# Context loads queued ahead of the last store of expert answers, and a merge moved one step earlier

## The reference, cut to what matters

```python
x = x + L0_xattn(layernorm(x), ctx, Wq, Wk, Wv, Wo, bo)            # 16 heads of 64
x = x + L0_ffn(layernorm(x), gate_w, w1, b1, w2, b2, sw1, ...)     # one of 2 experts, and a shared one
x = x + L1_xattn(layernorm(x), ctx, ctx, mask)                     # softmax(x ctx^T / 16) ctx, one head
x = x + L1_ffn(layernorm(x), weight_int8, weight_scale, bias)      # int8 product of 256 x 256
```

## Time and profile before

| | us |
|---|---|
| median of 3 runs | 957.77 |
| lowest, highest | 957.72, 958.77 |
| the profiled execution | 958.77 |
| its span | 956.0 |

### The profile page before, as it was taken

The page is one execution under the profiler, slowest core; times in us unless marked ns, Lnnn a source line. Parts: engine busy times, 40 slices in busy tenths (PEclk is TensorE's granted clock), DMA queues, the critical chain, the costliest instruction groups (busy, mean ns, idle before and its releaser), DMA issues.

```text
span 956.0 us, 19821 instructions
## 1 busy us (share of the span) xinstructions
PE 903.7 (95%) x6730; PEld 794.5 (83%) x6730; DVE 623.0 (65%) x1634; ACT 525.6 (55%) x1258; POOL 268.2 (28%) x337
## 2 busy tenths in 40 slices
PE   5889999999999999999999999998989999998864
PEld 4779888898888988889898898887878999996643
DVE  6766666767667676676766767665654666348777
ACT  4655565555655556555565555654742555446633
POOL 1323333333333333333433334333100000041214
PEclk9999999999999999999999999999999999999985
DMA  9230000000000000000000000000550142265502
GB/s 290 97 106 17 2 18 5 21 16 5 16 5 21 16 5 16 5 21 16 5 16 5 21 14 7 0 5 9 162 190 20 54 169 85 63 193 163 155 6 77
DMA packets 29459, 50.56 MB, mean 53 GB/s; under 512 B 2480, under 2 KB 24080, under 8 KB 27648
## 3 DMA queue, kind: packets, MB, share of 16 engines
q1 hardware_dynamic: 27888, 46.42, 15.6%
q0 software_dynamic: 1536, 3.67, 1.3%
HBM read 41.83 MB, written 8.26 MB: 52 GB/s over the span
## 4 chain that ended last, share of the span: by engine, by line
PE 88%; DVE 7%; ACT 2%; issue 2%; DMA 1%; POOL 0%; DVEq 0%
PE bank L1648 27%; PE bank L1677 10%; PE bank L1841 9%; PE bank L1696 9%; PE bank L1861 8%; PE bank L1662 8%; PE bank L1630 6%; PE bank L1717 5%; PE bank L1950 2%; PE bank L1968 1%; DVE norm_stats L1023 1%; PE bank L1811 1%; PE bank L1609 1%; PE bank L1957 1%; DMA x_all<-in_x 1%
## 5 line engine op out<-in xcount | busy, mean ns | idle before, releaser
L664 POOL TENSOR_TENSOR probs<-probs,row_rcp 112x375 f32<-112x375 f32 x256 | 202.4, 813 | 415.8 <-DVE row_rcp L1118 415.3
L784 ACT ACTIVATE probs<-bank,neg_max 112x375 f32<-112x375 f32 x256 | 144.4, 570 | 69.0 <-DVE neg_max L1112 68.9
L1677 PE MATMUL bank<-ident,probs 112*125 112x112 f32 x768 | 129.1, 277 | 2.3 <-DVE probs_t L1123 2.3
L1677 PEld LDWEIGHTS bank<-ident,probs 112*125 112x125 f32 x768 | 113.8, 187 | 18.2 <-issue 3.3
L1112 DVE TENSOR_REDUCE neg_max<-bank 112x1 f32<-112x375 f32 x256 | 123.3, 539 | 7.6 <-PE bank L1662 7.5
L1123 DVE COPY probs_t<-bank 125x336 f32<-125x336 f32 x128 | 64.7, 506 | 70.1 <-PE bank L1677 66.8
L756 ACT ACTIVATE k_parts<-bank 128x376 fp32r<-128x376 f32 x128 | 62.1, 485 | 69.3 <-PE bank L1648 69.3
L1648 PE MATMUL bank<-ctx_hi,wk_hi 128*128 128x376 f32 x256 | 97.2, 380 | 2.3 <-DVE k_parts L1103 1.5
L759 ACT ACTIVATE v<-bank 125x512 f32<-125x512 f32 x96 | 57.4, 598 | 57.2 <-PE bank L1648 57.1
L1696 PE MATMUL bank<-probs_t,v 125*64 125x112 f32 x1536 | 87.7, 263 | 0.6 <-ACT probs_t L772 0.6
L1696 PEld LDWEIGHTS bank<-probs_t,v 125*64 125x64 f32 x1536 | 74.0, 137 | 16.9 <-issue 16.7
(11 more groups left out here) (208 smaller groups left out, 1877.0 us busy)
## 6 DMA issues: line engine op xcount, KB each, us to landing
stage<-in_ffn_up SPq DMA_DIRECT2D x6, 1024.0 KB, 5.4
stage<-in_ffn_down SPq DMA_DIRECT2D x6, 1024.0 KB, 7.5
ctx_raw<-in_ctx_t SPq DMA_DIRECT2D x16, 375.0 KB, 3.4
ring_late<-in_ctx_t SPq DMA_DIRECT2D x10, 375.0 KB, 6.8
ring_late<-in_ctx_n SPq DMA_DIRECT2D x10, 375.0 KB
routed<-xn SPq DMA_DIRECT2D x1, 2240.0 KB, 11.1
rows_in<-routed SPq DMA_DIRECT2D x5, 448.0 KB, 6.1
answers<-y_rows SPq DMA_DIRECT2D x10, 224.0 KB, 2.7
```

The costliest lines, as they stand in the source:

```text
L664: eng.tensor_tensor(probs[s][:, :], probs[s][:, :], row_rcp[:, s:s + 1].broadcast_to([S, C]), ALU.mult).then_inc(probs_ready, 1)
L784: eng.activation(probs[r][:, :], SCORE_BANKS[i][0:S, 0:C], ACT.Exp, bias=neg_max[:, r:r + 1], accum_out=row_sum[:, r:r + 1]).then_inc(exp_ ...
L1677: t = eng.transpose(turn_bank(i, project)[0:CJ, j * S:(j + 1) * S], probs[QUAD * v + i][:, j * CJ:(j + 1) * CJ], ident[0:S, 0:S])
```

## The change

There are two moves; no operation is added or taken away. SyncE's `load_ring` of t = 3 to 6 now stands ahead of the wait for the last slot and of `store_rows(4)`, right behind `load_ring(2)`. In VectorE's last segment `norm3_merge(0)` and `norm3_stats(0)` stand in step 2, behind its `hid_lo`, and no longer in step 3; the moments and the first five small operations stay in step 3.

```diff
@@ SyncE @@
             load_ring(1)
             eng.wait_ge(down_ready, FIRST_SLOT + SLOTS - 1)
             store_rows(3)
-            load_ring(2)
+            for t in range(2, 2 + len(ring_late)):
+                load_ring(t)
             eng.wait_ge(down_ready, FIRST_SLOT + SLOTS)
             store_rows(4)
-            for t in range(3, 2 + len(ring_late)):
-                load_ring(t)
@@ VectorE @@
                     if s == NS - 1:
-                        if m == 3:
+                        if m == 2:
                             norm3_merge(0)
                             norm3_stats(0)
+                        if m == 3:
                             norm3_moments(0)
                             norm3_ops(0, 0, 5)
```

## The result

The changed kernel takes **968.03 us** (median of six, 963.14 to 971.12) beside **957.50 us** for the kernel before (median of six, 956.69 to 958.77).

The account below looks back on a forecast made before the run. TensorE's matmul queue was taken as the bound, busy 95% of 956.0 us. Merge +4.5 and `hid_lo` +0.6 gave +5.1, clock counted 0, on the median 957.8: 962.9 us; range 959.5 to 968.0.

Parts of the forecast that it names:

- What bounds the kernel: Whole kernel: TensorE busy 95% of 956.0 us, time won or lost where it stops or VectorE sets the pace.
- the held store: SyncE's queue: last store waits behind ring loads, landing about 851.2 instead of 839; merge begins 4.5 us later.
- The ring time of 4.8 us: SyncE's queue: time per ring for rings 3 to 6 without gathers, ends 4.5 and 6.2; last byte at 850.3 us.
- one more `hid_lo`, +0.6: VectorE, between merge and ready normalisation: one more `hid_lo` of 0.62 us, adding 0.6 us.
- I count 0: TensorE behind its new stop: low clock costs nothing, since some 24 matmuls (5 us) end ahead of the delayed `xn`.
- the stated end of 1.7: TensorE behind its stop: at most 1.7 us lost to low clock, counted only in the high end.
- A: Rival, SyncE's queue: the store is not held up; gain of at most 0.75 us, 957.0 to 957.8, chance 0.07.
- B: Rival, SyncE's queue: rings drain fast enough, 3.5 us each; +0.4 us, 958.2, chance 0.06.
- C: Rival: SyncE blocks on stores or rings take 6 us, clock loss uncovered; +9 to +12, 967 to 970, chance 0.05.
- D: Rival, the attention: runs quicker with less traffic beside it, faster by more than 0.2%; chance 0.02.
- 0.75 us: Last feed-forward segment: the earlier merge, if its data were there, shrinks TensorE's two gaps by 0.75 us at best.
- B's sum of +0.4: Merge at m=2 under fast ring drain: group 0 a few tenths behind 853.3, plus one more `hid_lo`, sum +0.4.

Follow-up runs that it names:

- e1_rings_only: The kernel before with only the loads of rings 3 to 6 moved ahead of the last store, merge left at m=3: 963.63 us, ratio 1.0053.
- e3_store_on_act: The changed kernel with the last two `answers` stores issued by ScalarE on its own queue: 959.68 us, ratio 0.9998.
- e8: The changed kernel, nothing altered, run again on another chip: 967.11 us, ratio 1.0077 against the kernel before.
- the filler: The changed kernel plus 22 matmuls with unread results ahead of the waiting `down`; measured twice, 961.91 us (ratio 1.0037) and 962.67 us (ratio 1.0066).
- e4: The changed kernel, nothing altered, run again beside the first experiments: 963.76 us, ratio 1.0045 against the kernel before.
- e6: The changed kernel with only rings 3 and 4 ahead of the last store, merge at m=2: 963.36 us, ratio 1.0033.
- e9: The changed kernel, nothing altered, run again on a third chip: 962.55 us, ratio 1.0057 against the kernel before.
- e10: The changed kernel plus 22 matmuls with unread results in TensorE's stop, on the third chip: 962.67 us, ratio 1.0066.
- e11: The kernel before plus 14 matmuls with unread results in TensorE's 2.89 us gap that ended at 710.73: 957.26 us, ratio 1.0002.
- e12: The kernel before with rings 3 and 4 moved ahead of the last store, merge left at m=3: 957.87 us, ratio 1.0003.
- e13a to c: The changed kernel, nothing altered, three profiled executions on a fourth chip: 961.55, 966.11 and 961.46 us.
- e14: The kernel before with rings 3 to 6 ahead of the last store and `ctx_n` loads cut into 112 and 13 partitions: 958.60 us, ratio 0.9993.
- e2: The kernel before with only the merge and statistics of group 0 moved to m=2: 957.55 us, ratio 0.9993.
- e5: The changed kernel plus 22 matmuls with unread results ahead of the `down` that waits: 961.91 us, ratio 1.0037.
- e7: The changed kernel with each `ctx_n` load cut into 112 and 13 partitions, merge at m=2: 961.81 us, ratio 1.0018.

## Why the prediction was right and where it was not

**What bounds the kernel; the held store (edit 1): right, and shown.** e1_rings_only has the whole loss, e3_store_on_act, which takes the store alone out of SyncE's queue, has none. The trace of after follows the forecast closely: the store issued at 840.93 (840.6 forecast), the first gather at 852.37 (852.2), the merge at 858.80 (858.8), `shift` at 865.25 (865.5), TensorE's stop of 4.47 us ahead of a `down` (about 5). The ring time of 4.8 us, taken as a choice between 4.5 and 6.2, was right for this execution; that the choice hit so closely was in part luck, since e8 has 2.4 us more.

**The term "one more `hid_lo`, +0.6": a little too large.** From merge to `shift` the trace has 6.45 us against 6.11 before, +0.34. In the times it is smaller still: the changed kernel and e1_rings_only differ by 0.13 us.

**The step that failed in the sum: "I count 0" for the clock, and all behind `shift`.** The claim was that the "some 24 matmuls" behind the stop end ahead of the delayed `xn` even at the low clock, and that from the merge on everything keeps its spacing. They don't: in the trace of after these 24 take 6.58 us (from 862.04 until TensorE turns `xn` at 868.62), with the filler, at full clock, 5.16 (860.86 to 866.02), and `xn` lies ready at 867.53. So TensorE comes last there, and the first `neg_max` is 0.60 later. The filler gives 9.26 back, in both of its runs, which shows the cause. I had the row that says so the earlier trace rows and argued it away. In e8, with 6.8 us low, the clock costs 1.26 us, which the stated end of 1.7 covers; the rest of its 2.7 is the pause of ScalarE, of which the forecast had nothing. On top of it came 0.8 us behind the first `neg_max` in this execution. In the other traces that stretch has two values, whatever the kernel: 86.3 to 86.5 us (before, e4, e6, e8, e9, e10, e11, e12, e13a to c, e14) and 86.9 to 87.2 (after, e1, e2, e3, e5, e7). So the 0.8 is not put down to the change; what decides between the two I don't know. The attention does keep its spacing, as claimed: its last `neg_max` follows the first by 50.4 or 50.5 us in before, after, e1 to e8 and e10, of either kind, so the 0.8 lies in the last block.

**The median: +10.5 where the trace has +6.2. This part is not settled.** The clock's 0.60 is a small part of the miss: of the 5.4 us between forecast and median, some 4 lie between the profiled execution and the median. On the chips of the experiments the same program lost 5.5, 8.2 and 5.2 us of the median; ratios 1.0045, 1.0077 and 1.0057. The forecast of +5.1 is a ratio of 1.0053, which lies inside the intervals of all three, and outside that of the first measurement alone. Two quantities vary, as the table shows, and the forecast had only part of either. One is the drain of the queue: the ends "4.5 and 6.2" a ring covered it, but the traces of before can't show how it varies. The other is low clock far ahead of the change. For the first measurement there are 25 executions of the changed kernel with a mean clock each: the median is 0.978 (0.982 in the profiled one, which is among the fastest) and the span falls by 0.8 us for each 0.001 of clock, so about 3 us of the extra go with the clock. It is not shown that the change lowers it: in the groups of e4, e8 and e9 the changed kernel's median clock is 0.980 to 0.982, that of the kernel before 0.981. At the clock of 0.982 its spans are 962.2 to 965.2; on the chips of e4 and e9 they are 960.4 to 962.3 and on that of e8 963.4 and 963.5. So up to another 3 us are not clock, and look as a drain like e8's would. Neither is shown for those executions, which have no trace of their own but one.

A part of it was in my own starting point. 957.5 is what six executions of the kernel before gave; on the four chips of the experiments its medians were 958.3, 959.0, 957.4 and 959.2. And its profiled execution carried a pause of ScalarE (1.68 us idle before the relu at 851.53, while the next relu's matmuls were done too, since it follows at 852.58 with no gap), so its stretch from store to `shift` is 37.89, where e11_before_filler and e12_two_ahead_merge3 have 36.7. Against those the changed kernel loses 5.5 us there, not 4.35. Taken up to the first `neg_max`, the traces whose store was not held (e2, e3, e11, e12, e14) need 45.8 to 46.2 us from the store, those of the changed kernel 51.1 to 52.5, and e8 56.5: a loss of 5 to 6.5 us, and in e8 of 10.5. So a late gather and a pause like those of e8 would make about the +10.5 of the first measurement; that its executions had them is not shown.

**The rivals.** A (not held) is refuted by the trace and e3. B (fast drain) did not happen here, but a fast drain does take most of the loss away: with edit 1 alone all of it (e14_split_merge3), with both edits, which is what B was about, not all in the median (e7_split_ctx_n, 1.0018 [0.9998, 1.0038]). The 145 GB/s that the Trainium skill's figure gave for five engines (DMA: Bandwidth & Descriptors, Specifications) are not reached: 119. C (+9 to +12) is where the median fell, but not by C's mechanism as far as the traces show. SyncE did block at the stores (4.12 us) and the clock was not covered (0.60 us); yet C had group 0 in at 863 to 864, and the merge began at 858.80 here and at 861.87 at the latest in any trace, so the number agrees and the path to it is not shown. What can be said is that 0.05 for a time there was small for a forecast that rested on one number of the drain out of one execution. D did not happen.

**Edit 2.** Alone it is worth nothing (e2: 0.9993 [0.9971, 1.0015]), although the forecast allowed 0.75 us: the merge begins earlier, but the first `neg_max` of e2 (872.07) and that of e12 (872.19), two executions with the same clock ahead of it, are 0.1 us apart. With the store late by a little it may do harm: e6 1.0033 against e12 1.0003, e7 1.0018 against e14 0.9993. Each of these pairs spans two chips, and the intervals overlap, so this is not shown; and e3 has the merge at m=2 too, behind a longer wait, and lost nothing (0.9998). The wait ahead of `hid_lo` is therefore not enough. What e6 and e7 have in their traces, and e3, e12 and e14 have not, is ScalarE's 4.60 us. Why ScalarE stands there is open: the trace names only the bank that it reads, and the matmuls into it were over by 857.99 in e7, 3.6 us ahead of the relu.

**Slips in the working that moved nothing.** Rings 0 and 1 were not alone from 803.89 on: other loads move some 300 GB/s until about 804.5, and the rings' own traffic begins at 805.2, which is the 1.3 us of the estimate. B's sum of +0.4 does not follow from its own terms: a merge at about 853.6 and 0.6 more behind it make -0.1.

## What to carry to other kernels

A store whose data somebody waits for must not be queued behind loads that nobody needs yet; price such a reorder by the time at which the queue is empty, and look whether another engine's queue is free. An operation moved ahead in an in-order engine brings all its waits with it, so its slack is what counts, not its length. A forecast out of one profiled execution needs the spread of what it exposes: here the drain of a queue that was hidden, and the clock behind every new stop. And low clock beside a loss is not yet its cause: follow the chain mark by mark, as in e8, where more than half of what seemed clock was a pause of another engine.

## What the runs showed of the hardware that I had not expected

- Once about two rings are queued, SyncE's issue of the next `ctx_t` blocks: for 3.3 to 4.7 us in the kernels with rings 3 to 6 ahead of the store, up to 5.66 in the kernel before, while the `ctx_n` issue behind it takes 0.6 to 1.1. With `ctx_n` cut into 112 and 13 partitions, every issue of e14 takes 0.45 to 0.64 us, but for the first (2.19) and one of 0.88.
- The same queue of the same program took 28.4 to 30.0 us from store to first gather on four occasions and 31.6 us on a fifth. Whether that belongs to the chip or to the single execution is open: e3, on the chip of e8, had its second blocked issue over in 3.50 us, as the traces elsewhere (3.4 to 3.6), where e8 took 4.16.
- In four traces (before, e6, e7, e8) ScalarE started an instruction 1.7 to 3.7 us after its input was ready and it was free, and nothing in them says why.
- A stop of 3.5 to 5.1 us of TensorE went with 3.4 us of granted clock at 1.2 GHz, one of 6.78 with 6.8 us (e1_rings_only, with 3.90, had 6.8 too, and yet its `neg_max` came only 0.58 us later: 1.9 us of them fell in the stop itself, and TensorE had 12 matmuls fewer to do before it turned `xn`).
- Stretches of 3.4 or 6.8 us at 1.2 GHz come at the same few places of the run (about 42, 70, 660 and 712 us) in some executions and not in others, for all these kernels, and are most of the scatter of the span: 3.4 to 17.0 us of them went with spans of 959.2 to 964.4 of one program on one chip.
